# A scratch of backward weight words relaid by weight tile: one 512 KB load for a gate or up tile in place of eight of 64 KB

## The reference, cut to what matters

```python
def dequant_gptq(qweight, scales, zeros, groupsize):     # 8 nibbles of K in one int32 word
    q = qweight[k // PACK, :] >> (k % PACK * 4)[:, None] & 15
    z = zeros[:, n // PACK] >> (n % PACK * 4)[None, :] & 15
    return q * s[g] - (z + 1) * s[g]                      # g = k // 128

gate, up = x2 @ Wg, x2 @ Wu                               # 1024 -> 2752
inter = gate * sigmoid(gate) * up
out = (inter @ Wd).astype(float16)                        # 2752 -> 1024
x = x + out
```

## Time and profile before

| | |
|---|---|
| median of three runs | 1228.19 us |
| the profiled execution: its time | 1226.89 us |
| its span | 1225.1 us |
| TensorE matmul busy | 1171.0 us, 96% |
| VectorE / ScalarE busy | 891.4 us, 73% / 849.6 us, 69% |
| DMA queue of SP | 147894 packets, 164.59 MB, 46.3% of 16 engines |

### The profile page before, as it was taken

One profiled execution on the slowest core, in us unless ns is written; L12 is line 12 of the kernel. 1 busy time (PEld: TensorE's weight loads), 2 busy tenths in 40 slices (PEclk: granted clock), 3 DMA queues, 4 the chain that ended last, 5 costly groups with the idle time before them and its releaser, 6 DMA issues.

```text
span 1225.1 us, 15458 instructions
## 1 busy us (share of the span) xinstructions
PE 1171.0 (96%) x5546; PEld 952.1 (78%) x5546; DVE 891.4 (73%) x935; ACT 849.6 (69%) x1390; POOL 206.2 (17%) x121
## 2 busy tenths in 40 slices
PE   4899999899999999999999799999999999999996
PEld 3799998678878788788788578778788788787873
DVE  6768723577777777777777798787777777777777
ACT  5612203878878788788788687778788787887862
POOL 0031100121121121111211761211211211211110
PEclk9999999899999999999999899999999999999995
DMA  8575874743533433434333355645434334334404
GB/s 287 177 290 165 297 223 145 182 112 91 119 104 94 119 97 106 114 94 121 100 96 94 103 158 139 180 151 151 108 93 123 104 91 120 100 101 112 141 28 179
DMA packets 148002, 165.61 MB, mean 135 GB/s; under 512 B 24838, under 2 KB 111046, under 8 KB 147670
## 3 DMA queue, kind: packets, MB, share of 16 engines
q1 hardware_dynamic: 147894, 164.59, 46.3%
q0 software_dynamic: 32, 0.03, 0.0%
HBM read 155.74 MB, written 11.64 MB: 137 GB/s over the span
## 4 chain that ended last, share of the span: by engine, by line
PE 82%; DVE 8%; DMA 3%; SPq 3%; issue 3%; ACT 1%; DVEq 0%
PE pair L1074 24%; PE pair L1041 24%; PE pair L1056 24%; PE pair L1001 8%; DMA x_fin<-in_x_dram 2%; SPq L370 2%; DVE acc L868 1%; PE pair L961 1%; DVE q_in L815 1%; DVE p L625 1%; DMA u_all<-in_x_dram 1%; DMA z_in<-zeros_plus_one 1%; DVE s_r L625 0%; ACT u_all L536 0%; DVE y_nat L774 0%
## 5 line engine op out<-in xcount | busy, mean ns | idle before, releaser
L868 DVE SCALAR_TENSOR_TENSOR acc<-pair,s_down,acc 128x1024 f32<-128x1024 f32 x336 | 430.9, 1283 | 216.9 <-PE pair L1074 216.5
L568 ACT ACTIVATE pair<-pair,ratio 128x512 f32<-128x512 f32 x616 | 383.1, 668 | 122.0 <-PE pair L1041 122.0
L587 ACT ACTIVATE pair<-pair,ratio 128x512 f32<-128x512 f32 x588 | 365.3, 660 | 135.9 <-PE pair L1056 135.8
L1041 PE MATMUL pair<-xs,wg 128*128 128x512 f32 x1408 | 392.0, 400 | 6.6 <-issue 5.3
L1056 PE MATMUL pair<-xs,wu 128*128 128x512 f32 x1344 | 373.5, 400 | 4.4 <-DVE sil L852 4.4
L1041 PEld LDWEIGHTS pair<-xs,wg 128*128 128x128 f32 x1408 | 263.8, 189 | 76.9 <-ACT pair L568 5.8
L1056 PEld LDWEIGHTS pair<-xs,wu 128*128 128x128 f32 x1344 | 250.2, 189 | 71.8 <-issue 14.3
L1074 PE MATMUL pair<-mid_h,wd 128*128 128x512 f32 x704 | 281.6, 404 | 6.8 <-DVE acc L868 4.1
L1074 PE MATMUL pair<-mid_l,wd 128*128 128x512 f32 x672 | 264.4, 393 | 0.0
L465 POOL CAST mid_h<-sil 128x1024 fp32r<-128x1024 f32 (+1 forms) x44 | 45.6, 1037 | 872.1 <-DVE sil L852 853.8
L1074 PEld LDWEIGHTS pair<-mid_h,wd 128*128 128x128 f32 x704 | 133.6, 191 | 45.8 <-DVE acc L868 10.9
(11 more groups left out here) (145 smaller groups left out, 369.3 us busy)
## 6 DMA issues: line engine op xcount, KB each, us to landing
q_in<-rows_backwards SPq DMA_DIRECT2D x672, 64.0 KB, 2.2
z_in<-zeros_plus_one SPq DMA_DIRECT2D x130, 256.0 KB, 4.5
toep<-kernel_padded SPq DMA_DIRECT2D x64, 512.0 KB, 6.2
q_in<-_L_ffn_down_qweight_dram SPq DMA_DIRECT2D x42, 512.0 KB, 5.7
u_all<-in_x_dram SPq DMA_DIRECT2D x16, 512.0 KB, 9.4
x_fin<-in_x_dram SPq DMA_DIRECT2D x12, 512.0 KB, 8.2
out_dram<-x_fin SPq DMA_DIRECT2D x12, 512.0 KB, 7.0
q_in<-in_x_dram SPq DMA_DIRECT2D x4, 512.0 KB, 5.3
```

Of the source, the lines that this page charges most:

```text
L568: act.activation(gate_ps[:, tb, :], gate_ps[:, tb, :], ACT.Copy, scale=ratio[:, 0, G * t + g:G * t + g + 1]).then_inc(gate_scaled, 1)
L587: act.activation(up_ps[:, tb, :], up_ps[:, tb, :], ACT.Copy, scale=ratio[:, 1, G * t + g:G * t + g + 1]).then_inc(up_scaled, 1)
L868: dve.scalar_tensor_tensor(out=acc[:, hid, :], in0=ps, scalar=scale, in1=acc[:, hid, :], op0=ALU.mult, op1=ALU.add).then_inc(down_taken, 1)
L1041: mm = pe.matmul(gate_ps[:, tb, :], w["g"][tau % 2][:, g, :], xs[:, part, g, 512 * tb:512 * tb + 512], start=g == 0 and part == 0, stop=pa ...
```

## The change

The scratch gets a layout by weight tile: 21 gate tiles, 21 up tiles and one tail tile that holds both, each tile as 16 word rows of 8 x 128 words (64 KB). Since a tile's 8 groups now lie behind each other in a row, `load_weights` reads it with one transfer, tail or not, with runs of 4 KB in place of 512 bytes. To fill the scratch, `turn_rows` issues two transfers for each weight and row set, one of 21 x 8 runs of 128 words and one of 8 runs of 64 words for the tail, 64 in all in place of 32. The count of parts that VectorE waits for is adapted.

```diff
-    rows_back = nc.dram_tensor("rows_backwards", (2, HID // PACK, INTER), I32, kind="Internal").ap()
+    rows_back = nc.dram_tensor("rows_backwards", (2 * TAIL + 1, 16, G, P), I32, kind="Internal").ap()
...
                 for e, q in ((0, gq), (1, uq)):
-                    sp.dma_start(bass.AP(rows_back.tensor, (e * (HID // PACK) + 15 - r) * INTER,
-                                         [[16 * INTER, G], [INTER // 2, 2], [1, INTER // 2]]),
-                                 bass.AP(q.tensor, r * INTER, [[16 * INTER, G], [INTER // 2, 2], [1, INTER // 2]])
+                    sp.dma_start(rows_back[e * TAIL:e * TAIL + TAIL, 15 - r],
+                                 bass.AP(q.tensor, r * INTER, [[P, TAIL], [16 * INTER, G], [1, P]])
+                                 ).then_inc(rows_back_in, 16)
+                    sp.dma_start(rows_back[2 * TAIL, 15 - r, :, M_TAIL * e:M_TAIL * e + M_TAIL],
+                                 bass.AP(q.tensor, r * INTER + P * TAIL, [[16 * INTER, G], [1, M_TAIL]])
                                  ).then_inc(rows_back_in, 16)
...
-                elif t == TAIL:
-                    for e in range(2):
-                        for g in range(G):
-                            sp.dma_start(q_in[slot][:, g, M_TAIL * e:M_TAIL * e + M_TAIL],
-                                         bass.AP(rows_back.tensor, e * (HID // PACK) * INTER + P * t + rows * g,
-                                                 [[INTER, 16], [0, PACK], [1, M_TAIL]])
-                                         ).then_inc(q_loaded[slot], 16)
                 else:
-                    e = "gu".index(m)
-                    for g in range(G):
-                        sp.dma_start(q_in[slot][:, g, :],
-                                     bass.AP(rows_back.tensor, e * (HID // PACK) * INTER + P * t + rows * g,
-                                             [[INTER, 16], [0, PACK], [1, P]])
-                                     ).then_inc(q_loaded[slot], 16)
+                    tile_at = 2 * TAIL if t == TAIL else "gu".index(m) * TAIL + t
+                    sp.dma_start(q_in[slot][:].rearrange("p g n -> p (g n)"),
+                                 bass.AP(rows_back.tensor, tile_at * 16 * G * P, [[G * P, 16], [0, PACK], [1, G * P]])
+                                 ).then_inc(q_loaded[slot], 16)
...
-                    sp.wait_ge(rows_back_in, 16 * 32)
+                    sp.wait_ge(rows_back_in, 16 * 64)
...
-                parts = (1 if m == "d" else G) * (1 + is_tail(tau)) + 1
+                parts = 1 + (m == "d" and is_tail(tau)) + 1
```

More of the change, by code:

```diff
@@ L349, in load_weights @@
                 loads += 1
-                rows = 16 * INTER
                 if m == "d" and t == TAIL:
```

## The result

The kernel after took 1221.66 us (median of 11 runs, 1217.3 to 1224.83) against 1228.19 us for the kernel before (11 runs): a ratio of 0.9944 with a 95% interval of 0.9932 to 0.9956. That is 6.5 us and 0.56% faster. The forecast was 1222.6. The experiments ran on four chips, on which the kernel before had medians from 1226.8 to 1228.6 us; each ratio is against the kernel before on the same chip, and a difference of medians from two chips can be off by one or two us. The profiled execution of after took 1221.8 us, with a span of 1220.0 at a granted clock of 0.981, 5.1 us less than the span before. Lines from L338 on stand about seven higher in the file than before: L1034, L1049 and L1067 are now the gate, up and down matmuls, L845 the product, L364 the load of a scratch tile, L391 the load for `x_fin`.

A forecast was written before the change was run, and what follows sets the result against it. TensorE's matmuls were taken to bound the kernel, some four fifths of the chain. Terms of 2.5 + 2.6 + 0.5 + 0 = 5.6 us took the profiled 1226.89 to 1221.3, plus 1.3 for the median: 1222.6 us, range 1218 to 1229.5.

The forecast's parts named there:

- Term one: FFN's start: down's words issued 9 us earlier, so step 0's product waits for ScalarE's gate function instead; 2.5 us won.
- Term two: Behind the FFN's start: with shorter TensorE waits the granted clock no longer falls; 2.6 us won, bounds 0 and 2.6.
- rival B: FFN's start: the clock still falls, so only 3.0 us are won, 1225.2 us; chance 22%.
- Term three: Second half's `x_fin` loads: earlier zeros ahead shorten TensorE's waits, the gate pair behind may share engines; 0.5 us won.
- The cap: Upper limit of the gain at the `x_fin` loads: TensorE's two waits, 1.96 + 0.45 = 2.4 us.
- rival E: Both `x_fin` waits vanish (2.4 in place of 0.5) beside the FFN's start gains: 7.5 us, 1220.7; chance 11%.
- Term four: Convolution: more copy issues and 512 byte runs fit in the time four heads take; cost 0, with 0.5 us possible.
- rival D: Convolution: short copies exceed the Toeplitz ring's room, deciding from 60 ns a packet; slower, 1245 at 90 ns; chance 11%.
- The seven engines: Convolution: a copy's 21 outer pieces are dealt to seven engines, three each; 96 packets to each per group, 3.1 us.
- The room I gave the ring: Convolution: Toeplitz loads go out seven heads (16 us) ahead and land in 6.1, leaving some 9 us of room.
- The rest: FFN's steady part: cheaper loads move nothing, since TensorE is busy throughout and SP is up to four tiles ahead.

The follow-up runs named there:

- the second two: The kernels before and after, each profiled a second time on one chip with no edit: 1228.39 and 1217.18 us, one execution each.
- the pieces behind that load: Against the kernel after, the gate tiles issued right behind the late `x_fin` loads (steps 28, 29) loaded in eight pieces: 1222.85 us, 0.9958 to before.
- the pieces ahead: Against the kernel after, the up tiles issued ahead of the late `x_fin` loads (steps 27, 28) loaded in eight pieces: 1225.79 us, 0.9977 to before.
- a second set: Against the kernel after, each 21 x 8 x 128 copy issued again to a scratch that nothing reads: 1235.55 us, 1.0064 to before.

## Why the prediction was right, and where its sum was not

The forecast, 1222.6 us with 1218 to 1229.5 and most of the chance within 0.5%, met 1221.66, just past that bound of 1222.0. Its mechanisms were all there. The sum of 5.6 us came out near the measured 6.5 partly by luck, because two terms were off in opposite directions.

- **Term one, down's load** (2.5 us): right. From the start of the gate matmuls of step 1 to that of up, TensorE needs 1.90 us where it needed 4.35: 2.45 us. The limit behind it was named rightly, ScalarE's gate function, and the product came at the 18.3 us forecast.
- **Term two, the clock** (2.6 us, bounds 0 and 2.6): too high. In the first execution of after 5.43 - 4.59 = 0.8 us were won, since the clock fell for a shorter time; the sign named for this term, PEclk at 1.00 in the windows behind the product, was absent there. Where it held, the stage took 58.93 us against 62.81 and 63.36, 3.9 to 4.4 for terms one and two together, not 5.1: in that execution TensorE, no longer behind, soon meets ScalarE's pace, and the later sets take up to 1.15 us where 0.94 was counted. The forecast and rival B are both true, in different executions; one wait without a fall, at 798.14, was too little to choose by.
- **Term three, the `x_fin` loads** (0.5 us, at most 2.4): the step that failed, mis-sized by a factor of five. The first two profiles give 2.9 us, the second two 2.6, and the medians about 2.5 to 3.8. The landing expected near 10 us was 8.3. I had seen the right cause, that the pair ahead goes out earlier, and then let the gate pair behind cancel most of it; the pieces behind that load changed nothing, the pieces ahead brought the waits back. The cap, the sum of the two waits, was also 0.5 us short of what came, for which no run shows the reason. That is rival E's half of the story.
- **Term four, the copies** (0): right in its result, with its parts off. SP's issues cost more than the 0.63 us taken: 0.77 for 21 x 8 x 128 and 0.65 for the tail columns, so a group's eight take 5.7 us (half of them in the timeline of after, below) where four took 2.5. A packet took 26 ns, under the 32 taken and far from the 60 from which rival D decides. The seven engines fit what the engines' share shows. TensorE waits for `toep` once, 2.5 us, as it did before the change. The room I gave the ring in rival D, 9 us, was not there for a second set, which cost 13.9 us where 4 to 6 were expected with that room.

```profile
127.23 0.77 SPq L338 DMA_DIRECT2D rows_backwards<-in_L_ffn_up_qweight_dram  x1
128.05 0.65 SPq L341 DMA_DIRECT2D rows_backwards<-in_L_ffn_up_qweight_dram  x1
128.74 0.77 SPq L338 DMA_DIRECT2D rows_backwards<-_L_ffn_gate_qweight_dram  x1
129.55 0.65 SPq L341 DMA_DIRECT2D rows_backwards<-_L_ffn_gate_qweight_dram  x1
```

- **The rest** (nothing in the steady part): right to 0.1 us of 388.

## What to carry to other kernels

Making transfers larger paid here where the queue that issues them is in the chain, and also where another load that is in the chain stands behind them: count what is still on the engines when that load is issued, and weigh what stands ahead of it over what follows. Ask what is late next before crediting a removed wait, and count a clock's fall as something that may or may not come, not as a yes or no. When a term is small because two effects are set against each other, forecast both ends, and keep a stage ledger by matmul number: it showed 0.1 us in 388 where totals spread by several us.

## What the runs showed that I had not expected

- A DRAM to DRAM copy in runs of 512 bytes takes 26 ns a packet, at 150 GB/s with about seven engines, less than the 32 ns of the loads in 512 byte pieces.
- The same kernel with the same waits (1.36 and 0.67 us) had its clock fall to the 1.2 GHz level in one execution and not in another.
- An SP issue of the same shape took 1.41 us where its like took 0.74, with the DMA engines at a share of 0.49; most likely it is held while the engines that it is dealt to are full.
- With a tensor of 4 bytes a partition more, the steady part takes 387.0 to 387.2 us in place of 387.9 to 388.1, in three executions out of three against none of eleven; the cause is open.
